# Local attention with four heads' sums in one bank, second products in channel quarters, and a new order of steps

## The reference, cut to what matters

```python
def l2norm(t):
    return t / jnp.clip(jnp.linalg.norm(t, axis=-1, keepdims=True), 1e-12)
...
h = shift_token(x)
q, k, v = jnp.split(h @ wqkv, 3, axis=-1)       # 8 heads of 64 channels
q, k = l2norm(q) * qs, l2norm(k) * ksc
q, k = rotary_xpos(q, k)
# windows of 128 queries, each against its own and the previous 128 keys
sim = jnp.einsum('bhwid,bhwjd->bhwij', bq, bk)  # bq holds q * 8
mask = (i < j) | (i > j + WINDOW) | (j == -1)
attn = jax.nn.softmax(jnp.where(mask, -big, sim), axis=-1)
o = jnp.einsum('bhwij,bhwjd->bhwid', attn, bv)
x = x + o @ wo
```

## Time and profile before

| | us |
|---|---|
| median of 3 runs (2029.45 to 2033.13) | 2031.3 |
| the profiled execution | 2031.94 |
| its span, first to last instruction | 2030.5 |
| PE busy over the span | 1801.4 (89%) |
| DVE, ACT, POOL busy | 1153.4, 939.2, 933.1 |
| mean granted TensorE clock | 0.919 |

### The profile page before, as it was taken

The page is one execution under the profiler, slowest core; times in us unless marked ns, Lnnn a source line. Parts: engine busy times, 40 slices in busy tenths (PEclk is TensorE's granted clock), DMA queues, the critical chain, the costliest instruction groups (busy, mean ns, idle before and its releaser), DMA issues. The chain is left out here.

```text
span 2030.5 us, 42787 instructions
## 1 busy us (share of the span) xinstructions
PE 1801.4 (89%) x14072; PEld 1357.6 (67%) x14072; DVE 1153.4 (57%) x2891; ACT 939.2 (46%) x1834; POOL 933.1 (46%) x919
## 2 busy tenths in 40 slices
PE   5999988889679999999979999599999999789887
PEld 4556655655357777777768888477777777577776
DVE  4556665656367776766523333776676666234343
ACT  2545555555335555455534444255545555333322
POOL 3345444554335565554423333355555555333433
PEclk7888888997779999999979999799999999799998
DMA  4333343333100000000121112100000000221221
GB/s 145 102 118 98 104 120 114 119 110 115 37 27 2 31 31 31 31 31 21 49 58 42 62 62 93 43 11 31 31 31 31 31 21 21 64 73 55 79 72 42
DMA packets 103736, 121.29 MB, mean 60 GB/s; under 512 B 23386, under 2 KB 75780, under 8 KB 103684
## 3 DMA queue, kind: packets, MB, share of 16 engines
q1 hardware_dynamic: 96772, 95.45, 15.7%
q0 software_dynamic: 6912, 25.17, 3.5%
HBM read 82.55 MB, written 37.77 MB: 59 GB/s over the span
## 5 line engine op out<-in xcount | busy, mean ns | idle before, releaser
L468 DVE TENSOR_REDUCE a_negm<-a_x 128x2 f32<-128x256 f32 (+3 forms) x256 | 202.8, 814 | 142.3 <-PE a_x L594 139.8
L864 POOL TENSOR_TENSOR work<-work 128x512 f32<-128x512 f32 x128 | 164.5, 1285 | 196.7 <-DVE work L1014 195.1
L430 ACT ACTIVATE a_PT<-a_c 128x384 f32<-128x384 f32 (+1 forms) x384 | 183.8, 522 | 140.8 <-PE a_c L633 87.7
L1539 DVE SCALAR_TENSOR_TENSOR m_hid<-m_a,mw_b,m_gate 128x512 f32<-128x512 f32 x96 | 71.9, 749 | 244.9 <-ACT m_gate L1477 220.8
L1032 DVE CUSTOM_DVE_ANT_0 l_x<-l_x,window 128x256 f32<-128x256 f32 (+1 forms) x512 | 183.9, 419 | 41.2 <-PE l_x L1129 40.9
L1063 PE MATMUL l_f<-w_hi,tails 128*128 128x512 f32 x384 | 170.6, 444 | 15.4 <-DVE work L1014 12.3
L1434 POOL TENSOR_TENSOR m_hid_lo<-m_hid,m_hid_hi 128x512 fp32r<-128x512 f32 x80 | 102.7, 1291 | 132.2 <-ACT m_hid_hi L1488 132.0
L941 ACT ACTIVATE l_PT<-l_c 128x512 f32<-128x512 f32 (+1 forms) x256 | 124.5, 538 | 74.4 <-PE l_c L1169 74.4
L1064 PE MATMUL l_f<-w_hi,tails 128*128 128x512 f32 x384 | 155.4, 405 | 0.0
L1065 PE MATMUL l_f<-w_lo,tails 128*128 128x512 f32 x384 | 154.2, 402 | 0.0
L878 POOL TENSOR_TENSOR l_PS<-l_PT 128x768 f32<-128x768 f32 x64 | 119.5, 1867 | 66.1 <-ACT l_PT L941 66.1
(11 more groups left out here) (239 smaller groups left out, 5140.8 us busy)
## 6 DMA issues: line engine op xcount, KB each, us to landing
a_Q<-qk_parts SPq DMA_DIRECT2D x192, 64.0 KB, 2.1
a_K<-qk_parts SPq DMA_DIRECT2D x192, 64.0 KB, 2.1
qk_parts<-a_qk_hi SPq DMA_DIRECT2D x32, 256.0 KB, 2.1
qk_parts<-a_qk_lo SPq DMA_DIRECT2D x32, 256.0 KB, 2.1
after_attn<-rows_out POOLq DMA_DIRECT2D x16, 512.0 KB, 5.3
xin<-after_attn SPq DMA_DIRECT2D x32, 256.0 KB, 3.1
m_xr<-after_attn SPq DMA_DIRECT2D x16, 512.0 KB, 4.1
xin<-in_L_attn_x SPq DMA_DIRECT2D x8, 512.0 KB, 3.5
```

The lines of the kernel that those rows point to most:

```text
L430: nc.scalar.activation(PT[:, p // PG % 2, 2 * (p % PG) + hh, QOFF[t]:QOFF[t] + nq], SC[hh][:, 0:nq], ACT.Exp, scale=AD ** -0.5).then_inc(e ...
L468: dve.tensor_reduce(negm[:, q, 2 * p:2 * p + 2], MX[i % 2][:, :, 0:nk], AX.X, ALU.max, negate=True).then_inc(max_done, 1)
L864: pool.tensor_tensor(t1[:, par, w, :], t1[:, par, w, :], t2[:, par, w, :], ALU.add)\
```

## The change

Six things change, all in the local attention:

1. `pv`: the two heads' products, 64 channels each, become four products of 32 channels. `OB` now holds rows of 32: half 0 of head 0, half 0 of head 1, half 1 of head 0, half 1 of head 1. The rows of `wo` are loaded in that order, by four DMAs of 32 partitions in place of one.
2. `sv`: it runs once per two pairs (`GROUPS` = 2, so `sv:0` and `sv:1`), as four products of 512 columns, each head's sums in 32 rows of `SB`. For this `PS` also holds the first query block, which POOL copies in `ps` with an instruction of its own.
3. `z`: it runs once per two pairs: one logarithm of `SB`, then four exponentials of 64 rows, which copy each pair's reciprocals into both halves of its `rr`. The second two wait for the first two.
4. DVE's clamp of the square sums goes. ACT does `relu(ss - 1e-24)` and then `ln(x + 1e-24)`: one small ACT instruction more per block, one DVE instruction fewer.
5. Waits follow the new counts: `sv:g` needs `ps` of both its pairs, `zn:p` also needs its `pv`, `pv:p+1` still needs `zn:p`.
6. `STEPS` is written in another order.

```diff
         STEPS = [s.rsplit(":", 1) for s in """
-            f_x:0 f_xe:0 sm:4 st:0 f_qk:0 sm:5 f_qe:0 st:1 ps:0 f_qk:1 f_qe:1 f_iv:0 sm:6 st:2 f_qk:2 pv:0 f_qk:3
-            f_qe:2 sv:0 f_qe:3 z:0 sm:7 st:3 ps:1 f_qk:4 f_iv:1 f_qe:4 f_qk:5 xr:0 mt:1 f_qe:5 f_iv:2 st:4 f_qk:6
-            f_qk:7 pv:1 zn:0 f_qe:6 f_qe:7 f_iv:3 st:5 sv:1 ps:2 z:1 st:6 pv:2 zn:1 zs:0 f_t:0 zs:1 f_te:0 sv:2
-            f_sm:0 z:2 f_t:1 zn:2 f_te:1 st:7 f_sm:1 f_t:2 f_te:2 ps:3 pv:3 zs:2 f_sm:2 f_t:3 sv:3 f_te:3 z:3 f_sm:3
-            f_v:0 zn:3 f_v:1 zs:3 f_v:2 f_mt:0 f_v:3 out:0""".split()]
+            f_x:0 f_xe:0 sm:4 st:0 f_qk:0 f_qe:0 sm:5 st:1 f_qk:1 ps:0 f_qe:1 f_iv:0 f_qk:2 sm:6 f_qe:2 st:2 f_qk:3
+            f_qe:3 sm:7 st:3 ps:1 f_qk:4 f_qk:5 f_iv:1 f_qe:4 f_qe:5 f_iv:2 mt:1 pv:0 f_qk:6 f_qe:6 sv:0 z:0 zn:0
+            f_qk:7 f_qe:7 st:4 pv:1 f_iv:3 st:5 ps:2 zn:1 st:6 pv:2 f_t:0 f_te:0 st:7 f_sm:0 xr:0 f_t:1 f_te:1
+            f_sm:1 f_t:2 ps:3 f_te:2 sv:1 z:1 f_sm:2 zn:2 f_t:3 zs:0 f_te:3 f_sm:3 pv:3 zs:1 zs:2 f_v:0 zn:3 f_v:1
+            f_mt:0 zs:3 f_v:2 f_v:3 out:0""".split()]
...
+                        pool.tensor_copy(PS[:, i % 2, :, 0, :], PT[:, i % 2, :, 0, 0:P]).then_inc(ps_done, 1)
+                        pool.tensor_tensor(PS[:, i % 2, :, 1:TB, :], PT[:, i % 2, :, 1:TB, 0:P],
+                                           PT[:, i % 2, :, 0:TB - 1, P:2 * P], ALU.add).then_inc(ps_done, 1)
...
-                        nc.scalar.activation(inv[:, par, :], ss[:, par, :], ACT.Ln).then_inc(log_done, 1)
+                        nc.scalar.activation(inv[:, par, :], ss[:, par, :], ACT.Relu, bias=least[:, 0:1])\
+                            .then_inc(log_done, 1)
+                        act.wait_ge(log_done, 2 * n + 1)
+                        nc.scalar.activation(inv[:, par, :], inv[:, par, :], ACT.Ln, bias=least[:, 1:2])\
+                            .then_inc(log_done, 1)
...
+                        act.wait_ge(s_full, b * GROUPS + i + 1)
+                        act.wait_ge(z_done, b * PAIRS + 2 * i)
+                        logs = rr[:, 1, :]
+                        nc.scalar.activation(logs, SB[:, :], ACT.Ln).then_inc(ln_done, 1)
+                        act.wait_ge(ln_done, b * GROUPS + i + 1)
+
+                        for pp in range(2):
+                            if pp == 1:
+                                act.wait_ge(rr_done, 4 * (b * GROUPS + i) + 2)
+                            for half in range(2):
+                                nc.scalar.activation(rr[FD * half:FD * half + FD, pp, :],
+                                                     logs[FD * pp:FD * pp + FD, :], ACT.Exp, scale=-1.0)                                    .then_inc(rr_done, 1)
...
-                        if w == 1:
-                            dve.wait_ge(ss_raw, b * 8 + i + 1)
-                            dve.tensor_tensor(ss[:, par, :], ss[:, par, :], least[:, :], ALU.max)\
-                                .then_inc(ss_done, 1)
...
                             nq = P if j == TB - 1 else 2 * P
+                            for half in range(2):
+                                for hh in range(2):
+                                    at, c = FD * half + Q4 * hh, FD * (2 * i + hh) + Q4 * half
+                                    m = pe.matmul(OB[at:at + Q4, P * j:P * j + nq], V[:, j, c:c + Q4],
+                                                  PT[:, i % 2, hh, j, 0:nq], start=(j == 0), stop=(j == TB - 1),
+                                                  skip_group_check=True)
...
+                        pe.wait_ge(ps_done, 4 * (b * GROUPS + i + 1))
...
+                                at = FD * pp + Q4 * hh
+                                m = pe.matmul(SB[at:at + Q4, :].rearrange("p (t q) -> p t q", q=P), ones[:, :],
+                                              PS[:, pp, hh, :, :], start=True, stop=True, skip_group_check=True)
```

More of the change, by code:

```diff
@@ L704, in load @@
             sp.dma_start(raw[k], self.wqkv[P * k:P * k + P]).then_inc(self.loaded, 16)
-        sp.dma_start(wo, self.wo_w.rearrange("(k p) n -> p k n", p=P)).then_inc(self.loaded, 16)
+        rows = self.wo_w.rearrange("(k e h d) n -> h e d k n", e=2, h=2, d=FD // 2)
+        for half in range(2):
+            for hh in range(2):
+                at = FD * half + FD // 2 * hh
+                sp.dma_start(wo[at:at + FD // 2], rows[half][hh]).then_inc(self.loaded, 16)
     def first(self, sp):
@@ L751, in local_attention @@
         LOW = 32
+        Q4 = P // 4
         negm = sb("negm", [P, TB, 2, P])
@@ L1135, in do @@
                         pe.wait_ge(max_done, 2 * (b * UNITS + 4 * i + 4))
-                        pe.wait_ge(ln_done, b * PAIRS + i)
+                        if i == 0:
+                            pe.wait_ge(ln_done, b * GROUPS)
+                        else:
+                            pe.wait_ge(mrow_done, b * 2 + 1)
                         if name == "f_mt" and not isinstance(b, int):
@@ new lines, in do @@
+                            for half in range(2):
+                                for hh in range(2):
+                                    at, c = FD * half + Q4 * hh, FD * (2 * i + hh) + Q4 * half
+                                    m = pe.matmul(OB[at:at + Q4, P * j:P * j + nq], V[:, j, c:c + Q4],
+                                                  PT[:, i % 2, hh, j, 0:nq], start=(j == 0), stop=(j == TB - 1),
+                                                  skip_group_check=True)
+                        m.then_inc(o_full, 1)
+                    elif name == "sv":
+                        pe.wait_ge(ps_done, 4 * (b * GROUPS + i + 1))
+                        pe.wait_ge(ln_done, b * GROUPS + i)
+                        pe.wait_ge(mrow_done, b * 2 + 2)
+                        pe.wait_ge(y_done, b * TB)
+                        for pp in range(2):
+                            for hh in range(2):
+                                at = FD * pp + Q4 * hh
+                                m = pe.matmul(SB[at:at + Q4, :].rearrange("p (t q) -> p t q", q=P), ones[:, :],
+                                              PS[:, pp, hh, :, :], start=True, stop=True, skip_group_check=True)
+                        m.then_inc(s_full, 1)
```

56 lines of the change are left out of this document (18 added, 38 removed).

## The result

The changed kernel is slower: 2045.95 us (median of 5 runs, 2042.42 to 2046.79) against 2033.13 us (5 runs, 2029.45 to 2034.21) of the kernel before on the same chip; ratio 1.0067, 95% interval 1.0055 to 1.008. The prediction was 2023. The profiled execution of the changed kernel took 2046.79 us (span 2045.3), 14.85 us more than the one of before.

A forecast was written before the change was run, and what follows sets the result against it. PE was taken to bound the local attention's loops. Front -1.4, back +0.5, tail +0.1 make -0.8 us a turn, -11 over 14 turns; ends +5, first fills -2: -8 on 2031.9, so 2023 us, range 2000 to 2042.

The forecast's parts named there:

- PE's saved work: Loop turn: four `sv` become two, `pv` about unchanged; PE's work falls 2.14 us a turn, if nothing waits.
- The gap between `st:5` and `st:6`: Front: `st:6` starts 2.62 us after `st:5`, waiting about 1.2 for exponentials; removing `sv:1` there saves nothing.
- The `mrow` and `pv:2` waits: Front: PE's 0.7 us wait for `mrow` and 0.5 us wait ahead of `pv:2` both go, per turn.
- The front: Turn from `f_x` to `f_t:0`, 33.3 us before: claimed to get 1.4 us shorter.
- the waits of the back: Between `f_t:0` and `f_v:0`: PE was to wait ahead of `f_sm:1`, `f_t:3` and `f_sm:3`.
- The back: Turn from `f_t:0` to `f_v:0`: 12.2 us against 11.7, +0.5, with DVE freeing the first bank at 12.1.
- slower rival: Back: late `ps:3` (past 6.45) or exponential pairs over 2.9 us delay `f_v:0`; 2050 us if 2 us late, chance 0.23.
- The ends: Last batches: one `zn`, one `pv` and perhaps weight preparations join the path; 2.4 us per layer, together +5.
- The tail: Turn from `f_v:0` to the next `f_x`, 11.8 us before: same steps, `zs:3` ready about when `out` wants it, +0.1.
- The clamp: Front: four clamps per turn leave DVE, which no longer holds `f_qk:7`; worth about 0.3 us a turn.

The follow-up runs named there:

- e5_old_parts_new_order: Kernel before with the clamp on ACT and the changed kernel's step order, keeping sums per pair and 64-channel products; 2067.41 us, ratio 1.0170.
- e7_sv1_short: Kernel before in its own order, `sv:1` cut to two bf16 products of ones (pair 1's sums not computed); 2030.3 us, ratio 1.0005.
- e3_zs0: Changed kernel with one step moved, `zs:0` behind `f_te:3` instead of ahead of it; 2036.19 us, ratio 1.0028 to the kernel before.
- e10_last: Changed kernel with a separate step order for the last batch of each layer only; 2035.93 us, ratio 1.0033 to the kernel before.
- e1_clamp: Kernel before with only the clamp of the square sums moved from DVE to ACT; 2024.65 us, ratio 0.9976.

## Why the prediction was wrong, point by point

**Right.** PE's saved work: two `sv` at 1.00 us (forecast 0.95), `pv` at 1.65 (1.60 to 1.67), and e5_old_parts_new_order against the changed kernel shows it arriving, 1.9 of 2.14 us in turns at the full clock. The gap between `st:5` and `st:6`, 2.41 us with 0.96 of waiting (2.62 and 1.2): a removed `sv` there saves nothing, as e7_sv1_short showed in the old order. The `mrow` and `pv:2` waits went. The front, 32.1 for 31.9; `st:5` waits 0.33 for exponentials, which was not counted. The places of the waits of the back: `f_sm:1`, `f_sm:3` and `f_v:0`.

**The back, the first term that was mis-sized:** +0.5 was counted, +1.1 came. The path was the predicted one: ACT's block, then pair 3's high part, then DVE's split, which frees the bank. The lengths were not. From the start of `f_t:0` the logarithm began at 7.7 us (7.5 counted), logarithm and exponentials took 3.2 us (2.9), and from their end to the end of the split it was 1.9 us (1.7): 12.75 in place of 12.1, with no slack to take it up. So one of the slower rival's two conditions came, exponentials longer than 2.9 us; the other did not, for `ps:3` ended at 5.7 us and `sv:1` waited for nothing. e3_zs0 takes 0.5 us back with one step moved.

**The ends, the second one:** +5 was counted, +12.3 came (6.5 + 4.9, and 0.9 in `out`). The prediction put one `zn` and one `pv` on the path. It named `ps:3` but did not price the 3.24 us that `sv:1` waits for it. It also missed the half clock, at which that `pv` is 3.2 and the `sv` 1.9 us; that `pv:3` itself waited 2.80 us; and that ACT's and DVE's weight pieces and three of POOL's subtractions, 5.99 us, queue behind it. The earlier trace rows showed two of these, the 3.25 us `pv` and the 1.43 us pieces. e10_last and e5_old_parts_new_order show that it needs the form and this order together.

**The tail and the front, smaller ones.** The tail was counted at +0.1; it came at +0.3 in layer 0 and +0.6 in layer 1, of which 0.17 us lie ahead of `out` and the rest in `out`'s own products. Why these take longer no run shows. The front gained 1.15 us of the 1.4 counted, for the wait of `st:5`.

**The clamp** was counted as 0.3 us a turn in the front. In e1_clamp it is there (33.3 to 33.0 us), but the tail gets 0.12 us longer in layer 0 and 0.23 in layer 1, so that a turn gains 0.15 us in the one and nothing in the other.

**Sum.** 14 turns at +0.4 on the mean in place of -0.8 are 17 us (the back 8.5, the tail 5, the front 3.5), the ends 7 more, the start and fills 1 less: that is the 23 us between forecast and result in the profiled executions. The range ended at 2042, because the slower rival's 2050 was cut at part of its price. That rival came nearest to the time, but not by its own sum: it had +17 us in the loops and +3 at the ends, where +5.8 and +12.3 came.

## What to carry to other kernels

Taking work off the busiest engine is worth nothing where that work filled a gap between two steps that wait on each other elsewhere; find the gap's length first (start to start), then ask what is left to fill it. The same holds where another engine's row is as long as this one's up to the next hand-off, even if no wait shows yet. An order written for a steady loop has to be read once more for its last iteration, cut down to the steps that remain: there a regrouping that needs all partial results before the first final one can put the whole tail in a row. And where a forecast finds no slack, a few tenths of a microsecond in the lengths decide, and that fork wants a price of its own.

## What the runs showed of the hardware that was not expected

- Four tiles of 32 columns cost no more than two of 64: 32 matmuls in 1.65 us from start to start, where 16 took 1.67.
- VectorE and POOL stop each other until an instruction ends. In the rows of the last batch above, POOL's subtraction that starts at 1038.17 is over when the next starts, at 1040.33, and that one takes 2.61 us:

```profile
1040.33 2.61 POOL L895 TENSOR_TENSOR l_zl<-l_zt,l_zh 128x512 fp32r<-128x512 f32 x1
```

  Each is over 1.1 us after the end of DVE's weight piece (1039.24 and 1041.81), nearly the whole 1.27 us that it takes undisturbed; and DVE's second piece, which starts while POOL's first runs, takes 2.05 for 1.64. The clamp behind POOL's addition is the same. The Trainium skill, "SBUF — State Buffer", section SBUF: two separate sides, calls it an exclusive lock on a shared pair of ports, taken by DVE instructions with two SBUF inputs against GpSimd ones that read SBUF: whoever starts first has it to the end. The rows above agree.
- Four exponentials of 64 rows took 2.59 us, 0.65 each, as long as one of 128 rows (0.63): half the rows save nothing.
- The kernel with fewer waits in a stretch can have the lower clock: from 1340 to 1670 us PE waits 20.0 us in the changed kernel, always at a granted clock of 1.00, and 16 us in e5_old_parts_new_order, which falls to 0.50 five times there, once behind ten microseconds in which PE was busy for 8.2. Turns with such a stretch are 0.3 to 1.5 us longer than those without.
